# Where the kept rows are stored, gathered and added at the end of a perceiver layer with experts

## The reference, cut to what matters

```python
logits = x_flat @ gate_w.T
scores = softmax(logits)
_, topk_ids = top_k(scores, 2)
w = scores * one_hot(topk_ids, 8).sum(axis=1)
gu = einsum('nh,eih->nei', x_flat, experts_gate_up)      # x_flat: 512 x 512, 704 hidden
h = silu(g) * u
expert_out = einsum('nei,ehi->neh', h, experts_down)
out = einsum('neh,ne->nh', expert_out, w) + shared_weight * shared
x = x + out
```

## Time and profile before

| | |
|---|---|
| median of three runs | 699.43 us (698.73 to 699.55) |
| profiled execution | 699.79 us |
| its span on the core | 697.9 us |
| PE busy | 689.4 us, 99% of the span |
| DVE busy | 557.1 us, 80% |
| ACT busy | 339.6 us, 49% |
| POOL busy | 206.9 us, 30% |
| DMA | 130.70 MB, mean 187 GB/s |

### The profile page before, as it was taken

How to read it: one execution, slowest core, us unless ns; L and a number is a source line. 1 busy time by engine, 2 the same in 40 slices (tenths; PEclk the granted TensorE clock), 3 DMA queues, 4 the chain that set the end, 5 groups by cost and what they waited for, 6 DMA issues and landing times.

```text
span 697.9 us, 9875 instructions
## 1 busy us (share of the span) xinstructions
PE 689.4 (99%) x3197; PEld 568.8 (81%) x3197; DVE 557.1 (80%) x723; ACT 339.6 (49%) x454; POOL 206.9 (30%) x154
## 2 busy tenths in 40 slices
PE   8999999999999999999999999999999999999997
PEld 7788888887888788888888888878888888878885
DVE  5688888878989998899996753769435798999997
ACT  4322222222245565556663333642233587878872
POOL 5844445454430000000000001226784111211235
PEclk9999999999999999999999999999999999999999
DMA  8056677766742237432210612514200899999994
GB/s 310 9 172 224 213 232 229 249 229 231 238 137 91 92 120 278 152 113 90 90 60 0 246 42 79 234 56 161 91 1 2 297 346 379 368 392 362 392 337 150
DMA packets 38974, 130.70 MB, mean 187 GB/s; under 512 B 6690, under 2 KB 10788, under 8 KB 35876
## 3 DMA queue, kind: packets, MB, share of 16 engines
q1 hardware_dynamic: 36548, 124.72, 50.0%
q0 software_dynamic: 1536, 4.20, 1.9%
q10 hardware_dynamic: 864, 1.44, 0.6%
HBM read 120.89 MB, written 9.46 MB: 187 GB/s over the span
## 4 chain that ended last, share of the span: by engine, by line
PE 81%; DMA 6%; DVE 5%; issue 3%; ACT 3%; POOL 2%; POOLq 0%; DVEq 0%; SPq 0%
PE ps L1041 25%; PE ps L991 8%; PE ps L992 8%; PE ps L995 8%; PE ps L883 4%; PE ps L884 4%; PE ps L885 4%; PE ps L1235 4%; DMA raw_u<-up_in 4%; ACT wu_hi L740 2%; PE ps L899 2%; PE ps L946 2%; DVE wu_lo L1803 1%; POOL met L531 1%; PE ps L1168 1%
## 5 line engine op out<-in xcount | busy, mean ns | idle before, releaser
L461 POOL TENSOR_TENSOR c_lo<-ring,c_hi 128x512 fp32r<-128x512 f32 x64 | 85.1, 1330 | 90.1 <-ACT c_hi L608 90.1
L608 ACT ACTIVATE c_hi<-ring 128x512 fp32r<-128x512 f32 x64 | 40.4, 634 | 128.4 <-PE ps L995 106.6
L478 POOL TENSOR_TENSOR w_lo<-raw,w_hi 128x1024 fp32r<-128x1024 f32 x11 | 26.7, 2426 | 250.5 <-ACT w_hi L727 237.0
L991 PE MATMUL ps<-qk_hi,c_hi 128*128 128x512 f32 x256 | 100.7, 393 | 0.0
L992 PE MATMUL ps<-qk_lo,c_hi 128*128 128x512 f32 x256 | 99.7, 389 | 0.0
L1471 DVE TENSOR_TENSOR runmax<-runmax,att 128x512 f32<-128x512 f32 x64 | 90.9, 1420 | 3.9
L995 PE MATMUL ps<-qk_hi,c_lo 128*128 128x512 f32 x256 | 68.6, 389 | 0.0
L1465 DVE SCALAR_TENSOR_TENSOR att<-ring,beta,ps 128x512 f32 (+1 forms) x64 | 47.8, 747 | 23.6 <-PE ps L995 23.1
L1041 PE MATMUL ps<-p_hi,d_hi 128*128 128x512 f32 x256 | 64.2, 393 | 0.1
L1041 PE MATMUL ps<-p_hi,d_lo 128*128 128x512 f32 x256 | 63.3, 389 | 0.0
L1041 PE MATMUL ps<-p_lo,d_hi 128*128 128x512 f32 x256 | 63.2, 389 | 0.0
(11 more groups left out here) (324 smaller groups left out, 1501.5 us busy)
## 6 DMA issues: line engine op xcount, KB each, us to landing
ring<-stream SPq DMA_DIRECT2D x64, 512.0 KB, 3.8
raw_u<-up_in SPq DMA_DIRECT2D x22, 1024.0 KB, 7.3
raw_d<-down_in SPq DMA_DIRECT2D x33, 512.0 KB, 8.0
ring<-ctx_in SPq DMA_DIRECT2D x32, 512.0 KB, 3.3
raw<-shared_in SPq DMA_DIRECT2D x11, 768.0 KB, 6.1
raw_u<-up_last_in SPq DMA_DIRECT2D x11, 768.0 KB, 7.8
slots<-blank SPq DMA_DIRECT2D x15, 256.0 KB
late<-wqkv_in SPq DMA_DIRECT2D x1, 3072.0 KB, 10.7
```

The lines of the kernel that those rows point to most:

```text
L461: pool.tensor_tensor(c_lo[:, s % 2, :], ring1[:, s, 0, :], c_hi[:, s % 2, :].bitcast(F32), ALU.subtract).then_inc(lo1_ready, 1)
L608: act.activation(c_hi[:, s % 2, :], ring1[:, s, 0, :], ACT.Copy).then_inc(hi1_ready, 1)
L991: pe.matmul(ps[:, s, :], hi, qk_hi[:, k, :], start=(k == 0), stop=False)
```

## The change

- The store of kept rows moves from SP's list to ACT's: in unit u it stands right behind the high part of the next unit's first up tile, and stores the rows of unit u-1. `keep` now multiplies by the row's weight (read from `info_all`, for which ACT waits once, before the first unit), so what lies in `slots` is weighted.
- The first four gathers add into `x` itself by DMA; `met` holds only the second four.
- POOL's loop of low parts ends one unit earlier. It waits for the last store, does the one-column add, issues the first gather, does its last low part, and then issues the other seven gathers.
- DVE's weighted adds of the first gather go; its two of the second gather become plain adds and wait for all first gathers too. ACT's scaling of the last two goes; POOL adds them once all have landed.
- The last unit's down products are made in two column halves, into two banks (2 and 1), each half's last signal its own. High and low parts of the output are made by halves, and the scatter runs half 0 high, half 0 low, half 1 high, half 1 low. The eight small products between them go.

```diff
-                if not second:
-                    sp.wait_ge(y_ready, u - 1)
-                    sp.dma_start(slots[bass.ds((u - 2) * P, P), :], y_out[:, :]).then_inc(y_stored, 16)
...
+            def gather_first(first, last):
                 for st in range(first, last):
+                    pool.indirect_dma_start(x[:, st, :], None, slots,
+                                            bass.IndirectOffsetOnAxis(kept_of[:, 0, st:st + 1], 0),
+                                            compute_op=ALU.add).then_inc(met_full, 16)
...
             final = pool.value_load(more[0:1, 0:1], min_val=0, max_val=MORE) + (E - 1)
-            with pool.Fori(1, final) as e:
+            with pool.Fori(1, final - 1) as e:
                 down_last_low(e)
             pool.wait_ge(y_stored, (final - 1) * 16)
             pool.tensor_tensor(blank[:, 0:1], blank[:, 0:1], blank[:, 1:2], ALU.add)
-            gather_kept(0, 0, ST, met_full)
-            gather_kept(1, 0, 2, met_second)
-            gather_kept(1, 2, ST, met_rest)
-            pool.wait_ge(added, 2 * ST)
+            pool.wait_ge(added, ST)
+            gather_first(0, 1)
+            down_last_low(final - 1)
+            gather_first(1, ST)
+            gather_second(0, 2, met_second)
+            gather_second(2, ST, met_rest)
+            pool.wait_ge(met_full, 16 * ST)
+            pool.wait_ge(met_rest, 16 * 2)
             for st in range(2, ST):
-                pool.wait_ge(met_step, st - 1)
-                pool.tensor_tensor(x[:, st, :], x[:, st, :], met[:, 1, st, :], ALU.add).then_inc(met_added, 1)
+                pool.tensor_tensor(x[:, st, :], x[:, st, :], met[:, st, :], ALU.add).then_inc(met_added, 1)
...
-                act.activation(y_out[:, :], ps[:, 2, :], ACT.Copy).then_inc(y_ready, 1)
+                act.activation(y_out[:, :], ps[:, 2, :], ACT.Copy,
+                               scale=info_all[:, bass.ds(u, 1), 1:2].rearrange("p a c -> p (a c)")).then_inc(y_ready, 1)
+
+            def store_kept(u):
+                act.wait_ge(y_ready, u + 1)
+                act.dma_start(slots[bass.ds(u * P, P), :], y_out[:, :]).then_inc(y_stored, 16)
...
+            def last_output_high(u, h):
+                act.wait_ge(y_psum_e, u * CH + (CH + h))
+                act.activation(y_hi[:, half_columns[h]], last_output(h), ACT.Copy, scale=info_s[:, 1:2]).then_inc(y_hi_ready, 1)
...
                 if not last:
                     up_high(u + 1, 0)
+                    if not first:
+                        store_kept(u - 1)
                 silu_e(u, 1)
...
+            def down_halves(u, c):
...
+                for h in range(2):
+                    to, cut = last_output(h), half_columns[h]
+                    for t in range(2 if c < 2 else 1):
+                        hi, lo = (part[:, c, t * P:(t + 1) * P] for part in (hh_e, hl_e))
+                        for i, (a, b) in enumerate(((hi, wd_hi), (hi, wd_lo), (lo, wd_hi))):
+                            mm = pe.matmul(to, a, b[c][:, t, cut], start=(c == 0 and t == 0 and i == 0), stop=False)
+                    if c == 2:
+                        pe.matmul(to, hh_e[:, 2, P:2 * P], wd_hi[2][:, 1, cut], start=False, stop=False)
+                        pe.matmul(to, hh_e[:, 2, P:2 * P], wd_lo[2][:, 1, cut], start=False, stop=True).then_inc(y_psum_e, 1)
...
+            def scatter_last():
+                pe.wait_ge(back_ready, 2)
+                for h, cut in enumerate(half_columns):
+                    for part, ready in ((y_hi, y_hi_ready), (y_lo, y_lo_ready)):
+                        pe.wait_ge(ready, 2 + h)
+                        for st in range(ST):
...
-                    add_met(0, 2, ST)
                     hidden_low(u, 2, last)
                     read_info(u)
                     way_back(1)
-                    add_met(1, 0, 2)
-                    output_low(1)
+                    add_met()
+                    last_output_low(0)
+                    last_output_low(1)
```

More of the change, by code:

```diff
@@ L39 @@
 WARM = 8
-WARM_END = 4
 WARM3 = (4, 3)
@@ L795, in unit @@
                     hidden_high(u, 2, last)
-                    output_high(u, 1)
+                    act.wait_ge(info_read, 2)
+                    last_output_high(u, 0)
+                    last_output_high(u, 1)
             shared_sides_high(0)
@@ L842, in _ @@
             act.wait_ge(down_done, 9 + CREDIT)
+            act.wait_ge(info_full, 16)
             unit(0, first=True)
@@ L849, in _ @@
             unit(final, last=True)
[L850 to L853, removed]
+            act.wait_ge(added, ST + 2 + 2)
             act.dma_start(out[P:2 * P, :], x[:, 1, :]).then_inc(out_stored, 16)
-            act.wait_ge(added, 2 * ST + 2 + 4)
+            act.wait_ge(added, ST + 2 + 4)
             act.dma_start(out[3 * P:S, 0:D // 2], x[:, 3, 0:D // 2]).then_inc(out_stored, 16)
@@ L1303, in unit @@
                 if last:
-                    scatter(0)
+                    scatter_first()
                 up(u, 2)
@@ L1310, in unit @@
                     pe.wait_ge(y_ready, u)
-                down(u, 0)
                 if last:
+                    down_halves(u, 0)
                     pe.wait_ge(hl_ready, u * CH + 2)
-                turn_hidden(u, 2, last)
-                down(u, 1)
-                if last:
-                    down(u, 2)
-                    keep_warm(WARM_END, 1)
-                    scatter(1)
+                    turn_hidden(u, 2, last)
+                    down_halves(u, 1)
+                    down_halves(u, 2)
+                    scatter_last()
+                else:
+                    down(u, 0)
+                    turn_hidden(u, 2)
+                    down(u, 1)
             def count_places():
@@ L1852, in output_low, with last_output_low, add_met @@
                                          op0=ALU.mult, op1=ALU.subtract).then_inc(y_lo_ready, 1)
-            def add_met(c, first, last):
-                if c == 0:
-                    dve.wait_ge(met_full, 16 * ST)
-                else:
-                    dve.wait_ge(met_second, 16 * 2)
-                dve.wait_ge(added, ST * (c + 1))
-                for st in range(first, last):
-                    dve.scalar_tensor_tensor(out=x[:, st, :], in0=met[:, c, st, :], scalar=weight_of[:, c, st:st + 1],
-                                             in1=x[:, st, :], op0=ALU.mult, op1=ALU.add).then_inc(added, 1)
+            def last_output_low(h):
+                dve.wait_ge(y_hi_ready, 2 + h)
+                cut = half_columns[h]
+                dve.scalar_tensor_tensor(out=y_lo[:, cut], in0=last_output(h), scalar=info_s[:, 1:2],
+                                         in1=y_hi[:, cut].bitcast(F32), op0=ALU.mult, op1=ALU.subtract).then_inc(y_lo_ready, 1)
+            def add_met():
+                dve.wait_ge(met_full, 16 * ST)
+                dve.wait_ge(met_second, 16 * 2)
+                for st in range(2):
+                    dve.tensor_tensor(x[:, st, :], x[:, st, :], met[:, st, :], ALU.add).then_inc(added, 1)
             def unit(u, first=False, next_to_last=False, last=False):
```

47 lines of the change are left out of this document (29 added, 18 removed).

## The result

The changed kernel takes 702.50 us (median of four executions, 701.67 to 702.84); the kernel before took 699.49 beside it (four, 698.73 to 699.71). The ratio is 1.0042, 95% interval 1.0031 to 1.0054: 3.0 us slower. The forecast was 1.45 us slower, so the loss is twice the one forecast. The profiled execution is the shortest of the four, 701.67 us at a span of 699.9; the other spans are 700.5, 701.1 and 701.0.

What follows compares the result with a forecast made beforehand. PE (TensorE) was taken to set the pace, with the closing gather chain arriving just in time. Span 697.9 + 0 (loop) + 1.6 (gather ahead) - 0.15 (halves) = 699.35; as time 699.43 + 1.45 = 700.9 us, range 699.2 to 703.0.

Steps and rivals of the forecast that it cites:

- The deciding term: GpSimd's first gather ahead of its last low part: low part and VectorE's up tile 1.6 us late, reaching the end.
- The bound for a landing after 672.9: VectorE starts its tile first, low part 675.6 to 678.0, PE waits 0.9 us, second half tile ends 679.1, 1.7 late.
- The mark of a low part at 673.3 to 674.2 or at 675.6: Sign of a right forecast: GpSimd's last low part starts at one of these times.
- the marks of a held tile: Sign of a right forecast: one of VectorE's two half tiles after 674 takes over 1.8 us.
- The landing: Last store on ScalarE's queue: issued about 669.1, landing 3.3 us later at 672.4, bounds 671.2 and 677.0.
- Rival C: Last store lands no earlier or is delayed, beyond 675; PE waits for the low part, up to +4.2: 703.6; chance 0.06.
- The loop at 0: Moving the store to ScalarE's queue changes the unit loop by 0 us, bounds -1.2 and +1.5.
- The gathers move nothing: Four adding gathers at the end land after 3.7 us, bounds 3.7 and 5.2; VectorE asks for them only near 689.
- The halves at -0.15: Last unit's output in column halves: worth -0.15 us, bounds -0.5 and +0.3.
- A: Second collision at the close: GpSimd's closing adds hold VectorE's adds of gathered tiles, 1.4 us late: 702.3; chance 0.22.
- B: Nothing displaced at 674.26 on VectorE: its tiles and the late low part fit together, price 0: 699.3; chance 0.15.
- D: Loop gains its idle 1.2 us and the tail 0.5, with no collision: 697.7; chance 0.04.

Runs made afterwards that it cites:

- e3: The kernel before with only GpSimd's order changed: wait for the store, one column, first plain gather, last low part, other seven gathers; 701.85 us, ratio 1.0043.
- e1: The changed kernel with the old order: GpSimd's last low part ahead of the store wait, all four adding gathers behind it; 700.54 us, ratio 1.0019.
- e11: The changed kernel with loads of the second and third up tiles cut to a quarter from the second unit on; 697.45 us.
- e12: The kernel before with the store on ScalarE's queue, a plain gather ahead of the low part, and the load cut of e11; 697.10 us.
- e2: The kernel before with only the store of kept rows moved to ScalarE's queue, unweighted; 699.27 us, ratio 1.0001.
- e6: The changed kernel, but after the wait for the store GpSimd runs the low part ahead of all gathers; 703.17 us, ratio 1.0048.
- e7: The changed kernel, but GpSimd's last low part also waits until the gather ahead of it has landed; 709.15 us, ratio 1.0149.
- e9: The changed kernel without the adding gathers and the new order: plain gathers, old order, store on ScalarE's queue, weighted rows, halves; 699.00 us, ratio 0.9991.
- e4: The kernel before with only the last unit's output in two column halves, without the eight small products; 699.81 us, ratio 1.0006.
- e8: The kernel before with the store on ScalarE's queue, weighted rows and plain adds, but plain gathers, old order, no halves; 699.35 us, ratio 0.9995.

## Why the prediction was right, and where it was not

The forecast was slower, 700.9 us, range 699.2 to 703.0. Slower came true, and 702.5 lies in the range, 1.6 us above the forecast; the loss is 3.0 us where I had 1.45.

**The deciding term.** The gather ahead of the low part was named as the term that decides, with the low part's collision with VectorE as the way, and a chain from there to the end. That holds: e3 alone has a loss of the same ratio, e1 gives back 2.0 us. I sized it at 1.6 us. By the clock of the two profiled executions the transposes came 2.09 us later (683.41 for 681.32), and measured from the last unit's start 3.37. The bound for a landing after 672.9 comes near by its times: low part from 675.6 to 678.0, held tile to 679.1. It ran from 676.0 to 678.4, and the tile ended at 679.5. The way was another, though. In that bound the low part is ready early and waits for VectorE's first half tile, begun at 674.26; in the run that half tile was done by 674.2, and the low part waited for the late landing, the one-column add and the gather. The mark of a low part at 673.3 to 674.2 or at 675.6 failed by 0.4 us; the marks of a held tile (4.78 us) and of PE waiting over 1 us (2.55) came true.

**The landing was the mis-sized term.** I had the store issued at 669.1, behind ScalarE's high part, and landing 3.3 us later. The rows of ScalarE:

```profile
664.70 0.69 ACT L768 ACTIVATE y_out<-ps,info_all 128x512 f32<-128x512 f32 x1
665.79 1.92 ACT L750 ACTIVATE wu_hi<-raw_u 128x2048 fp32r<-128x2048 f32 x1 [0.41 <-DMA raw_u<-up_in]
665.94 0.34 ACTq L773 DMA_DIRECT2D slots<-y_out  x1
```

The issue went out 0.15 us after that tile began, since it waits for nothing that the tile makes. It was 3.2 us earlier than I had it, and the landing took 7.4 us in place of 3.3. The errors nearly cancel, 673.3 for 672.4, and that is luck. My mark for this step, a landing 2.5 to 4 us after an issue near 669, failed on both counts. The row of before that I took as nearest, a gather on its own queue at 3.7 us, was the wrong one; the store behind SyncE's queue at 7.90 was. e11 and e12, with less queued, have 3.4, so it is the load on the DMA engines that makes the 7.4, not the store.

The Trainium skill, DMA: Bandwidth & Descriptors, section Queues, rings and completion order, has each DMA engine take turns between queue rows with work, and I leaned to an early landing by it. The packets by queue in the changed kernel (packets, MB, share of 16 engines), from 669 to 670 us and from 671 to 672:

```profile
q1 hardware_dynamic: 57, 0.34, 84.8%
q10 hardware_dynamic: 14, 0.03, 7.3%
...
q1 hardware_dynamic: 78, 0.32, 77.0%
q10 hardware_dynamic: 63, 0.11, 28.4%
```

q10, ScalarE's queue, moves its packets among those of q1, SyncE's, which agrees with the page. But no packet of it shows between 666 and 669 us, for 3 us behind the issue, and from 670 to 672 it has a quarter of the time (26.8 and 28.4%). Turns were no promise of an early landing.

**GpSimd's steps behind it.** The one-column add took 0.86 us where I had 0.15: it began inside the VectorE tile at 672.95 and ended 0.05 us after it, as I had it only in the bound for a landing before 672.1. The gather's issue took 1.64 us where I had 1.00, the price of a plain one. PE waited 2.55 us for the low part, where the forecast had this covered and the branch beside it had 0.9; the unit began 1.28 earlier than in the kernel before, and that makes up most of the difference. Rival C (landing late, PE waits for the low part, 703.6) had this wait, but wanted a landing beyond 675, which didn't come.

**The loop at 0** was right: e2, the store alone, has a ratio of 1.0001. The last unit's start differs by over 2 us between kernels that don't differ there (673.12 in the changed kernel, 674.49 in e1, 674.42 in e6, 672.37 in e7), so the 1.28 us of the changed kernel's profiled execution can't be called a gain of the store. ScalarE's issues are hidden altogether: nine of 0.34 us beside an ACTIVATE that keeps its 1.92.

**"The gathers move nothing"** was wrong in two places. They land after 5.6 us, above my bound of 5.2, and occupy GpSimd for 1.54 to 2.37 us each, the 2.37 with 0.9 us of a VectorE tile in front. In the changed kernel this is hidden, because PE is late anyway: VectorE's adds at 691.36 wait for nothing. With the old order (e1) they make VectorE wait 0.78 us, and stage 2 is 0.86 us longer than in e9. The Trainium skill, Collectives: The Full Stack, section The bandwidth ceiling, gives an adding transfer half the rate; the time from issue to landing here is 1.5 times that of a plain one before by the medians (5.6 and 3.7) and 1.3 times that of the plain ones behind it in the same kernel (4.3), and I had drawn nothing from it for the issue. No run shows the rate of the transfer alone.

**The halves at -0.15** can't be told from nothing: e4 has +0.24 us in stage 2, and e9 against e8 +0.10 there and -0.35 in the median. In e4 VectorE's closing adds waited 0.30 us for GpSimd's, which waited for ScalarE's scaling, and this for the landing of gathered rows.

**The rivals.** A, the second collision at the close, gave 702.3 and is nearest by its number, but it is not what happened: the two adds of gathered rows took 1.29 us for both, and GpSimd's adds began at 693.57, 0.9 us after VectorE's had ended. Slower gathers removed the clash, as my "against" had it. That the measured time lies next to A's is chance. B, no displacement, fell by the held tile. D, a gain of 1.7, had nothing to show: e9, with all of the change that can't displace the low part, gains 0.7 us against its runs of before, at the edge of the interval (0.9982 to 1.0000).

**The level.** For the profiled execution the sum gave 701.24, and it took 701.67. The other three took 0.6 to 1.2 us more, and I have no trace of them, so where the rest of the 1.6 us lies stays open. Open too is how the low part takes the port while its gather still runs. The records show only that it does so with the low part next in line (changed kernel, e3) and not without (e7); they don't show when GpSimd asks for it.

## What to carry to other kernels

Work that can't run beside another engine's often has a slot, here the 2.2 us between two of VectorE's up tiles, and the step in front of it is free only if it ends before the slot opens. Before putting a wait for a DMA ahead of such work, take the landing time of that DMA under the same load, with the longest row for its kind and not the one that looks most like it, add the full time of everything that comes in between, with the rest of the other engine's tile if it can start inside one, and compare with the slot's start. Letting a DMA add saves work on engines that had time to spare, and costs issue time and landing time on the queue that didn't.

## What the runs showed of the hardware

A VectorE subtraction of two SBUF tiles ran 1.23 us beside a running gather on GpSimd (e7), but was held for 4.78 and 3.83 us when a GpSimd subtraction stood right behind the gather, and ended about 1.1 us after that. The Trainium skill, SBUF — State Buffer, section Who interferes with whom, says that a VectorE instruction with two SBUF inputs contends with a GpSimd one that reads SBUF, and that issue order decides which of the two blocks. By the shown starts VectorE was first (674.72, against 675.43) and lost, so the order that counts isn't that of the records.

The other way round, a gather that starts inside a VectorE operation on two SBUF tiles takes about the rest of it longer. Plain ones took 0.94 to 1.00 us undisturbed and 1.84 with 0.97 us left (e3, 674.21); adding ones 1.54 to 1.64 undisturbed, 2.43 with 0.92 left (e11, 668.36), 2.67 with 1.17 left (e7, 672.28) and 2.71 with 1.28 left (e1, 677.88). One that starts ahead of the tile is not longer (1.00 in e12, from 667.88, with the tile at 668.26), and neither is the tile.

An issue on ScalarE's queue ran beside an ACTIVATE on the same engine (0.34 us from 665.94, inside 665.79 to 667.71).

PE stood for 5.71 us in e7, from 675.25 to 680.96, and by its end the granted clock was at half, 1.2 GHz; products of 512 columns then came every 0.43 us instead of 0.23, until 685.8. The windows of e7:

```profile
674.00:678.00 4.00, 1.25 (x6) 0.71 (x4) 3.96 (x5) 2.10 (x3) 0.95 (x1) 1.00 0.45 67
681.00:683.00 2.00, 2.00 (x5) 1.61 (x6) 0.00 (x0) 0.00 (x0) 1.70 (x2) 0.50 0.33 55
```

In the changed kernel, where PE stood for 2.55 us, it kept 1.00 to 696 us. So the longer wait cost more than its own length: e7's stage 1 is 4.7 us longer than the changed kernel's, with 3.2 us more of this wait.
